# Attention's stages in another order, and score chunks of 384 and 256 keys for 512 and 128

## The chip, the cores and the metric

The kernel runs on one core of one Trainium2 chip. The metric is the device time of one execution in microseconds (us). The core's engines are TensorE (PE in the profile; its weight loads are PEld), VectorE (DVE), ScalarE (ACT), GpSimd (POOL) and the queue of SyncE (SP), which issues nearly all transfers. Each engine works its instructions strictly in the order of its program and waits on semaphores that the others raise.

## The reference, cut to what matters

One transformer block with adaptive layer norm, on x of shape 2 x 2048 x 256, in float32:

```python
mod = (silu(c) @ wmod).reshape(2, 6, 1, -1)      # sa, ca, ga, sb, cb, gb; ga and gb kept at least 0.25 in size
h = layernorm(x) * (1 + ca) + sa
k, v, q = rope(h @ Wk.T), h @ Wv.T, rope(h @ Wq.T)         # 2 query heads of 128, one shared key and value head
w = softmax(where(causal, q @ k.T * 128 ** -0.5, -inf))
x = x + ga * (concat_heads(w @ v) @ Wo.T)
h = layernorm(x) * (1 + cb) + sb
gate = softmax(h @ Wg + bg) - sigmoid(h @ Wt + bt) * 0.125
w = normalised(gate * (gate >= 0))               # 8 experts, width 1024, all computed for every token
x = x + gb * sum_e(w_e * (gelu(h @ W1_e + b1_e) @ W2_e + b2_e))
```

## The kernel before, in words

The 4096 tokens are 32 tiles of 128. SEQ lists them in the order in which attention takes them: batch 0's tiles t = 0 to 13, then batch 1's t = 0 and 1 in turn with batch 0's 14 and 15, then the rest of batch 1; i is the place in SEQ, TIME[i] its t. A product that must be near float32 is made of three matmuls on a high and a low part (hi x hi, hi x lo, lo x hi).

Attention is cut into stages (kind, i, part), and each stage into its instructions on PE, ACT, DVE and POOL:

- pre: rows and columns from wmod; wq and wo: the split weights; norm, rstd, xa, aT: layer norm of a tile, scaling, and its transposition; qkv: the projection; rope (POOL) and rotT: rotation and transposition of q and k.
- S: scores of one head against one chunk of up to 512 keys (lines 962 to 964, into one of two score banks); M (DVE, lines 1622 and 1625): the negated scores to probs with their minimum, the last chunk with the causal mask added; N: the minimum over a row's chunks; E (ACT, line 1302): the exponential of a whole row; T: transposition of probs (line 972) and its copies; PV (lines 993 to 998); O and Y: output projection and residual (line 899 and on, 1529 and on).
- xb, bT: the second layer norm and its transposition; gate (line 887): the gate's logits for four tiles, 16 matmul records of 36 columns; G1 and G2: gate weights of a batch on DVE; traw, tsum, tlo and split: tokens and weights made ready for the experts.

Which stage follows which on each engine is not written out: the planner order_stages (line 288) simulates the four engines when the program is built, with the lengths and dependencies of parts_of, and always takes the stage with the least rank:

```python
rank = (start + patience[engine].get(kind, 0), start)
```

start is when it could begin; PATIENCE holds an allowance in ns per engine and kind, the same for all tiles. A large allowance lets other stages pass. The result, ORDER, is what the engines' programs loop over (lines 917, 1274, 1562 and 1970), with waits on semaphores whose values follow from each stage's place among its kind. M of a score stage must be done before the next but one S may write its bank. SP's program keeps its own order; its stores of x1 wait for Y.

idle_fill (line 342) reads from the plan where PE would be idle for over 600 ns in the first 40 us, and puts matmuls on a zeroed part of mask_sb there (line 920), which write columns of the PV bank that nothing reads.

After attention the expert part runs 128 steps on PE (from line 1048), each with 21 products and 24 matmuls of the second layer, in an order that is written out. Three attention-side stages of the last tile, and the last gate, are done within its first steps.

Of the kernel before, what the change touches and what calls it, by code (L numbers as in the profile page):

```python
# [8 lines left out]
ACT = mybir.ActivationFunctionType  # L9
AX_X = mybir.AxisListType.X  # L10

P = 128
B, T, D = 2, 2048, 256
HS, NH = 128, 2
E, FF = 8, 1024
# [25 lines left out]
XS, PBUF, SUM_SLOTS = 8, 2, 4  # L41
# [26 lines left out]
TIME = [t for _, t in SEQ]  # L68
# [29 lines left out]
def chunks_of(i):  # L98

    return TIME[i] // 4 + 1  # L100


def width_of(i, chunk):

    return min(512, (TIME[i] + 1) * P - chunk * 512)


def stages_by_kind():
# [46 lines left out]
def parts_of(stage):  # L155


    kind, i, g = stage
# [9 lines left out]
    if kind == "split":  # L168
        end = TILES - 1
        return [("POOL", SPLIT_PHASES[g], [("rope", end, 0, "POOL", 4500), ("rotT", end, 0, "PE"),  # L170
                                           ("S", end, 4 + chunks_of(end) - 1, "PE")])]
    if kind == "pre":
        what, b = PRE[i]
        late = {"rows": 0, "gates": 1, "cols": 2}[what]
        after = [("silu", 0, 0, "DVE"), ("wmod", late, 0, "SP")]
        if PRE_AFTER[i] is not None:
            after.append(("qkv", PRE_AFTER[i], 0, "PE"))
        return [("PE", 3600 if i == 2 else 1900, after),
                ("ACT", 600, [("pre", i, 0, "PE")]) if what == "gates" else ("DVE", 900, [("pre", i, 0, "PE")])]
    if kind == "wq":  # L180
        return [("ACT", 1250, [("wqkv", 0, 0, "SP")]), ("DVE", 1150, [("wq", 0, 0, "ACT")])]
# [3 lines left out]
    if kind == "norm":  # L185
        n = ok(i + AHEAD) + ok(i - BEHIND)
        after = [("rstd", i - 2, 0, "POOL"), ("xa", i - 2 + AHEAD, 0, "DVE"), ("xb", i - 2 - BEHIND, 0, "ACT"),
                 ("Y", i - BEHIND, 0, "DVE"), ("x", i + AHEAD, 0, "SP")]
# [32 lines left out]
    if kind == "S":  # L221
        chunk = g % 4
        after = [("rotT", i, 0, "DVE")]
        n = AT[stage] - 1
        if n >= S_BANKS:
            after.append(("M", *STAGES["S"][n - S_BANKS][1:], "DVE"))
        return [("PE", 3 * max(120, 0.443 * width_of(i, chunk))  + 110 * (chunk == chunks_of(i) - 1), after)]
    if kind == "M":
        after = [("S", i, g, "PE")]
        if i >= PBUF:  # L230
# [25 lines left out]
    if kind == "G1":  # L256
# [2 lines left out]


PATIENCE = {
# [7 lines left out]
    "POOL": {"xa": 1625, "rope": 2132, "norm": 1836, "rstd": 2160, "traw": 352, "split": -1582},  # L269
}  # L270
PASS_ON = {"PE": 260, "ACT": 120, "DVE": 120, "POOL": 130, "SP": 0}
T_READER = {"T": "ACT", "aT": "DVE", "bT": "ACT"}
M_READER = {"qkv": "ACT", "Y": "DVE", "rotT": "DVE", "gate": "DVE"}
# [2 lines left out]
def reader_of(stage):  # L276

    kind, i, _ = stage
    if kind == "pre":
        return "ACT" if PRE[i][0] == "gates" else "DVE"  # L280
    if kind == "T":
        return "DVE" if is_split(stage[2]) else "ACT"
    if kind == "qkv":
        return "DVE" if TIME[i] >= EARLY else "ACT"
    return T_READER[kind] if kind in T_READER else M_READER[kind]


def order_stages(patience):

    queues, free, orders = {}, {}, {}
    ends = dict(LOADED)
    for stages in STAGES.values():
        for stage in stages:
            for engine, length, after in parts_of(stage):
                queues.setdefault((engine, stage[0]), []).append(
                    (stage, length, [x for x in after if x[:3] in AT or x[:4] in LOADED]))
                free[engine], orders[engine] = 0.0, []
    heads = {q: 0 for q in queues}  # L300
    last_in = {"T": [None] * T_BANKS, "M": [None] * M_BANKS}
    turn = {"T": 0, "M": 0}
    data_ready = {}
    while heads:
        best = None
        for (engine, kind), n in heads.items():
            stage, length, after = queues[engine, kind][n]
            if (engine, kind, n) not in data_ready:
                if any(x[:4] not in ends for x in after):
                    continue  # L310
                data_ready[engine, kind, n] = max(
                    [0.0] + [ends[x[:4]] + (PASS_ON[x[3]] if x[3] != engine else 70 * (engine != "PE"))
                             + (x[4] if len(x) > 4 else 0) for x in after])
            start = max(free[engine], data_ready[engine, kind, n])
            banks = None
            if engine == "PE":
                banks = "T" if kind in T_READER else "M" if kind in M_READER or kind == "pre" else None
            if banks:
                was = last_in[banks][turn[banks] % len(last_in[banks])]
                if was:  # L320
                    if (*was, reader_of(was)) not in ends:
                        continue
                    start = max(start, ends[(*was, reader_of(was))] + 120)
            rank = (start + patience[engine].get(kind, 0), start)
            if best is None or rank < best[0]:
                best = (rank, engine, kind, stage, start, length, banks)
        _, engine, kind, stage, start, length, banks = best
        ends[(*stage, engine)] = free[engine] = start + length
        orders[engine].append(stage)
        if banks:  # L330
            last_in[banks][turn[banks] % len(last_in[banks])] = stage
            turn[banks] += 1
        heads[engine, kind] += 1
        if heads[engine, kind] == len(queues[engine, kind]):
            del heads[engine, kind]
    return orders, ends
# [5 lines left out]
def idle_fill():  # L342

    fill, free = {}, 1000.0
    for stage in ORDER["PE"]:
        length = next(n for engine, n, _ in parts_of(stage) if engine == "PE")
        gap = ENDS[(*stage, "PE")] - length - free
        free = ENDS[(*stage, "PE")]
        if free < FILL_UNTIL and gap > 600:
            fill[stage] = int(FILL_SHARE * gap / FILL_NS)  # L350
    return fill
# [19 lines left out]
def adaln_block(nc, x, wqkvT, woT, wgt, bgt, w1, b1, w2, b2, c, wmod, cos, sin, ident, mask, out):  # L371
# [6 lines left out]
    with outer:  # L378
# [337 lines left out]
        with nc.Block() as block:  # L716
# [128 lines left out]
            def _(pe):  # L845
# [71 lines left out]
                for stage in ORDER["PE"]:  # L917
# [31 lines left out]
                    elif kind == "S":  # L949
# [6 lines left out]
                        if n >= S_BANKS:  # L956
                            pe.wait_ge(dve_M, n + 1 - S_BANKS)
                        w, b = width_of(i, chunk), BATCH[i]
                        keys = slice(chunk * 512, chunk * 512 + w)
                        q1, q2 = (q[:, i % QS, h * P:(h + 1) * P] for q in (q_hi, q_lo))  # L960
                        o = score_bank(stage)
                        nc.tensor.matmul(o[:, 0:w], q1, k_hi[b][:, keys], start=True, stop=False)  # L962
# [488 lines left out]
            def _(dve):  # L1451
# [110 lines left out]
                for stage in ORDER["DVE"]:  # L1562
# [48 lines left out]
                    elif kind == "M":  # L1611
# [3 lines left out]
                        if i >= PBUF:  # L1615
                            dve.wait_ge(*done(pe_T, "T", i - PBUF, groups_of(i - PBUF) - 1))
                        w = width_of(i, chunk)
                        to, highest = probs[i % PBUF][:, h, chunk * 512:chunk * 512 + w], top[:, i % 2, h, chunk:chunk + 1]
                        if chunk == chunks_of(i) - 1:
                            if i == 0:  # L1620
                                dve.wait_ge(l_mask, 16)
# [510 lines left out]
```

## Time and profile before

| | |
|---|---|
| median of 3 runs | 1730.13 us (1728.48 to 1731.81) |
| the profiled execution's own time | 1729.62 us |
| its span, first to last instruction | 1727.8 us |
| PE busy | 1713.5 us (99%) |
| DVE, ACT, POOL busy | 1210.5, 1012.4, 1010.5 us (70, 59, 58%) |
| mean granted clock of PE | 0.998 |

Times in the profile are from the span's start. A row of instructions gives its line, engine, operation, the tiles it writes and reads, the shape, the count, busy time and mean duration, and behind these the engine's idle time just before and who released it. PE's matmuls are pipelined: the next starts before the last one's record ends, so what a matmul costs is read from one start to the next. A float32 matmul that is not split shows as two records.

### The profile page before, as it was taken

The numbers are of one execution on the slowest core, as the hardware profiler recorded it, in microseconds if no ns is written. First come the engines' busy times: TensorE is split into PE (matmuls) and PEld (weight loads), VectorE is DVE, ScalarE is ACT, GpSimd is POOL, SyncE is SP. The second block draws the span as 40 slices with busy tenths as digits, with TensorE's granted clock in tenths as the row PEclk, the third lists the DMA queues.
The fourth block names the chain that finished last, engine by engine and source line by source line (L and its number), as shares of the span: only waits on it lengthen the run. The fifth ranks groups of instructions, "written<-read, shape, count | busy, mean of one in ns | idle before, by whom it ended". The sixth has DMA issues, their size and how long they took to land.

```text
span 1727.8 us, 26572 instructions
## 1 busy us (share of the span) xinstructions
PE 1713.5 (99%) x8416; PEld 1442.7 (83%) x8416; DVE 1210.5 (70%) x2282; ACT 1012.4 (59%) x1834; POOL 1010.5 (58%) x1722
## 2 busy tenths in 40 slices
PE   8999999999999999999999999999999999999998
PEld 7899998998888888888888888888888888888887
DVE  6787778777676666666666678666666666666676
ACT  4767777666665555555555566555555555555554
POOL 6654565355345564748483949374847566574842
PEclk9999999999999999999999999999999999999999
DMA  4100010011111111111011111222312011111101
GB/s 115 32 23 17 30 31 20 10 57 45 25 50 26 50 37 37 37 37 49 28 47 36 55 21 37 62 71 76 110 25 49 26 49 37 37 37 37 37 13 50
DMA packets 91836, 72.05 MB, mean 42 GB/s; under 512 B 11825, under 2 KB 89905, under 8 KB 91697
## 3 DMA queue, kind: packets, MB, share of 16 engines
q1 hardware_dynamic: 91552, 70.29, 14.7%
q8 instruction: 68, 1.11, 0.3%
q14 instruction: 72, 0.58, 0.1%
q10 hardware_dynamic: 144, 0.07, 0.0%
HBM read 61.82 MB, written 8.52 MB: 41 GB/s over the span
## 4 chain that ended last, share of the span: by engine, by line
PE 94%; issue 1%; ACT 1%; DVE 1%; POOL 0%; DVEq 0%; ACTq 0%; POOLq 0%
PE bank L1094 13%; PE bank L1093 13%; PE bank L1092 13%; PE bank L1048 12%; PE bank L1049 11%; PE bank L1050 11%; PE bank L972 3%; PE bank L998 3%; PE bank L1012 2%; PE bank L963 2%; PE bank L964 2%; PE bank L962 2%; PE bank L994 1%; PE bank L993 1%; PE bank L995 1%
## 5 line engine op out<-in xcount | busy, mean ns | idle before, releaser
L1381 ACT ACTIVATE g_sb<-c_sb,b_cols 128x512 f32<-128x512 f32 x384 | 276.2, 719 | 397.6 <-DVE c_sb L1896 293.7
L1721 DVE TENSOR_TENSOR h_lo<-g_sb,h_hi 128x512 fp32r<-128x512 f32 x512 | 390.6, 783 | 102.7 <-ACT h_hi L1385 102.1
L1092 PE MATMUL bank<-h_hi,w_both 128*128 128x512 f32 x1024 | 398.8, 389 | 0.0
L1094 PE MATMUL bank<-h_lo,w_both 128*128 128x512 f32 x1024 | 398.7, 389 | 0.0
L1093 PE MATMUL bank<-h_hi,w_both 128*128 128x512 f32 x1024 | 398.4, 389 | 0.0
L2060 POOL TENSOR_TENSOR h2f<-h2f,y_sb 128x256 f32<-128x256 f32 x216 | 201.5, 965 | 284.7 <-DVE y_sb L1745 284.7
L1048 PE MATMUL bank<-t_hi,w_hi 128*128 128x512 f32 x896 | 352.4, 393 | 4.1 <-DVE p_u L1887 1.8
L1049 PE MATMUL bank<-t_lo,w_hi 128*128 128x512 f32 x896 | 349.3, 390 | 0.0
L1050 PE MATMUL bank<-t_hi,w_lo 128*128 128x512 f32 x896 | 349.2, 390 | 0.0
L1385 ACT ACTIVATE h_hi<-c_sb,b_cols 128x512 fp32r<-128x512 f32 x384 | 272.2, 709 | 0.0
L1092 PEld LDWEIGHTS bank<-h_hi,w_both 128*128 128x128 f32 x1024 | 192.2, 188 | 40.1
L1094 PEld LDWEIGHTS bank<-h_lo,w_both 128*128 128x128 f32 x1024 | 192.2, 188 | 40.1
L1093 PEld LDWEIGHTS bank<-h_hi,w_both 128*128 128x128 f32 x1024 | 192.2, 188 | 40.0
L1048 PEld LDWEIGHTS bank<-t_hi,w_hi 128*128 128x128 f32 x896 | 168.4, 188 | 44.0 <-ACT p_u L1417 4.0
L1050 PEld LDWEIGHTS bank<-t_hi,w_lo 128*128 128x128 f32 x896 | 168.5, 188 | 35.3
L1049 PEld LDWEIGHTS bank<-t_lo,w_hi 128*128 128x128 f32 x896 | 168.6, 188 | 33.6
L1381 ACT ACTIVATE g_sb<-bank,b_cols 128x512 f32<-128x512 f32 x128 | 88.2, 689 | 177.6 <-PE bank L1050 177.4
L1914 DVE TENSOR_TENSOR c_sb<-bank,u 128x512 f32<-128x512 f32 x128 | 88.3, 690 | 119.1 <-PE bank L1050 116.5
L1887 DVE TENSOR_TENSOR p_u<-bank,u 128x512 f32<-128x512 f32 x128 | 88.1, 688 | 107.5 <-PE bank L1050 107.2
L1896 DVE TENSOR_TENSOR c_sb<-bank,p_u 128x512 f32<-128x512 f32 x128 | 88.5, 691 | 84.4 <-PE bank L1050 71.5
L570 POOL TENSOR_TENSOR w_sums<-w_raw 128x128 f32<-128x128 f32 x64 | 49.4, 772 | 145.6 <-PE bank L1094 131.0
L603 POOL TENSOR_TENSOR w_lo<-w_sums,w_hi 128x256 fp32r<-128x256 f32 x128 | 94.7, 759 | 0.0
(204 smaller groups left out, 2942.5 us busy)
## 6 DMA issues: line engine op xcount, KB each, us to landing
w_raw<-w_dram SPq DMA_DIRECT2D x128, 256.0 KB, 3.0
g_rows<-gates_scratch SPq DMA_DIRECT2D x31, 512.0 KB, 8.6
x_sb<-x_dram SPq DMA_DIRECT2D x32, 128.0 KB, 2.3
x_scratch<-x_sb SPq DMA_DIRECT2D x32, 128.0 KB, 1.7
x_slabs<-x_scratch SPq DMA_DIRECT2D x4, 512.0 KB, 7.3
out_dram<-x_slabs SPq DMA_DIRECT2D x4, 512.0 KB, 3.3
h2f<-x_scratch SPq DMA_DIRECT2D x4, 512.0 KB, 3.9
wmod_raw<-wmod_dram SPq DMA_DIRECT2D x4, 256.0 KB, 3.8
```

The source lines that it names most:

```text
L603: last = nc.gpsimd.tensor_tensor(lo[:, 3 + 2 * i:5 + 2 * i, :], w_sums[:, 2 * i:2 * i + 2, :], hi[:, 3 + 2 * i:5 + 2 * i, :].bitcast(F32), ...
L1048: nc.tensor.matmul(bank, hi, t_hi[p][:, b_, :], start=start, stop=False, skip_group_check=True)
L1049: nc.tensor.matmul(bank, hi, t_lo[p][:, b_, :], start=False, stop=False, skip_group_check=True)
L1050: nc.tensor.matmul(bank, lo, t_hi[p][:, b_, :], start=False, stop=stop, skip_group_check=True).then_inc(pe_prod, 1)
L1092: nc.tensor.matmul(o, w_hi, h_hi[:, ring, :], start=first, stop=False, skip_group_check=True)
L1093: nc.tensor.matmul(o, w_lo, h_hi[:, ring, :], start=False, stop=False, skip_group_check=True)
L1094: done_ = nc.tensor.matmul(o, w_hi, h_lo[:, ring, :], start=False, stop=last, skip_group_check=True)
L1381: nc.scalar.activation(g_sb[:, m % 2, :], source, ACT.Gelu_apprx_tanh, bias=bias).then_inc(act_g, 1)
L1385: nc.scalar.activation(h_hi[:, m % RING, :], source, ACT.Gelu_apprx_tanh, bias=bias).then_inc(act_hi, 1)
L1721: nc.vector.tensor_tensor(h_lo[:, m % RING, :], g_sb[:, m % 2, :], h_hi[:, m % RING, :].bitcast(F32), ALU.subtract).then_inc(dve_lo, 1)
L1896: nc.vector.tensor_tensor(c_sb[:, 0, :], bank_h, p1_u3[:], ALU.add).then_inc(dve_c22, 1)
L2060: last = nc.gpsimd.tensor_tensor(acc[:, k, half], acc[:, k, half], y_sb[:, u, k, half], ALU.add)
```

## The change

Three edits of the plan's input and one of the work:

- Chunks. For tiles with t = 4, 8, 12 the last chunk had 128 keys behind chunks of 512. The last two are now of 384 and 256 keys. Numbers of chunks, matmuls and moves stay; only where a chunk begins (first_of) and how wide it is (width_of) change.
- Allowances. PATIENCE may hold four numbers for a kind, for tiles 0 to 5, 6 to 13, 14 to 19 and 20 to 31 of SEQ. All values are new, so every engine's order may change.
- Two lengths in the planner: the third pre stage 1900 ns for 3600, and S no longer 110 ns longer for a row's last chunk.
- idle_fill stops at the first PV stage.

```diff
--- before.py
+++ after.py
@@ -100,9 +100,17 @@
     return TIME[i] // 4 + 1
 
 
+def first_of(i, chunk):
+
+    end = (TIME[i] + 1) * P
+    if end % 512 == P and end > 512 and chunk == chunks_of(i) - 1:
+        return chunk * 512 - P
+    return min(chunk * 512, end)
+
+
 def width_of(i, chunk):
 
-    return min(512, (TIME[i] + 1) * P - chunk * 512)
+    return first_of(i, chunk + 1) - first_of(i, chunk)
 
 
 def stages_by_kind():
@@ -175,7 +183,7 @@
         after = [("silu", 0, 0, "DVE"), ("wmod", late, 0, "SP")]
         if PRE_AFTER[i] is not None:
             after.append(("qkv", PRE_AFTER[i], 0, "PE"))
-        return [("PE", 3600 if i == 2 else 1900, after),
+        return [("PE", 1900, after),
                 ("ACT", 600, [("pre", i, 0, "PE")]) if what == "gates" else ("DVE", 900, [("pre", i, 0, "PE")])]
     if kind == "wq":
         return [("ACT", 1250, [("wqkv", 0, 0, "SP")]), ("DVE", 1150, [("wq", 0, 0, "ACT")])]
@@ -224,7 +232,7 @@
         n = AT[stage] - 1
         if n >= S_BANKS:
             after.append(("M", *STAGES["S"][n - S_BANKS][1:], "DVE"))
-        return [("PE", 3 * max(120, 0.443 * width_of(i, chunk))  + 110 * (chunk == chunks_of(i) - 1), after)]
+        return [("PE", 3 * max(120, 0.443 * width_of(i, chunk)), after)]
     if kind == "M":
         after = [("S", i, g, "PE")]
         if i >= PBUF:
@@ -259,15 +267,30 @@
 
 
 PATIENCE = {
-    "PE": {"aT": 853, "bT": 900, "qkv": 1076, "rotT": 985, "Y": 940, "pre": 1334, "gate": 1978, "S": 975,
-            "T": 977, "PV": 1001},
-    "ACT": {"aT": -2637, "xb": -620, "bT": -4432, "qkv": 339, "rotT": -135, "O": -1231, "norm": -794,
-            "pre": -4154, "wq": -241, "G1": 2484, "traw": 1444, "tsum": -8852, "E": 940, "T": 349},
-    "DVE": {"xa": -3943, "aT": -1508, "qkv": -1657, "rotT": -6407, "O": -1114, "Y": -1222, "norm": 94,
-            "pre": -1071, "wq": 1020, "wo": 225, "G1": -3210, "G2": -3508, "gate": -4620, "tsum": 821,
-            "tlo": -79, "M": -3080, "N": -1556, "T": -671},
-    "POOL": {"xa": 1625, "rope": 2132, "norm": 1836, "rstd": 2160, "traw": 352, "split": -1582},
+    "PE": {
+        "aT": (1046, 560, 900, 645), "bT": (826, 852, 883, 892), "qkv": (1372, 1103, 989, 947),
+        "rotT": (1000, 953, 808, 766), "Y": (678, 870, 694, 861), "pre": 1773, "gate": 1103,
+        "S": (704, 921, 911, 924), "T": (687, 911, 792, 923), "PV": (1102, 957, 926, 943),
+    },
+    "ACT": {
+        "aT": (-1903, -1575, -5842, -1993), "xb": (-6689, -6451, -7197, -1747), "bT": (791, -6967, -65, -5604),
+        "qkv": (677, 223, -111, 263), "rotT": (-2707, -915, -5797, -6565), "O": (-1251, -2912, -4427, -2595),
+        "norm": (-4257, -640, -668, 477), "pre": -827, "wq": -2526, "G1": 1457, "traw": 1955, "tsum": 832,
+        "E": (941, 1123, 584, 624), "T": (345, 531, -57, 427),
+    },
+    "DVE": {
+        "xa": (-1542, -1696, -9691, -4382), "aT": (-4742, -7023, -8155, -7911), "qkv": (-7968, -5270, -3986, -7931),
+        "rotT": (-956, -7692, -291, -5939), "O": (-172, -2897, -497, -8190), "Y": (-3563, -9531, -4252, -634),
+        "norm": (-145, 16, -281, -166), "pre": -1944, "wq": -81, "wo": 305, "G1": 701, "G2": 533, "gate": -268,
+        "tsum": 681, "tlo": -2057, "M": (-407, -5314, -490, -5831), "N": (-511, -4937, -1346, -1579),
+        "T": (-2208, -1049, -1413, -1422),
+    },
+    "POOL": {
+        "xa": (3029, 1099, 890, 992), "rope": (2037, 2012, 2177, 1842), "norm": (1776, 2173, 1664, 1360),
+        "rstd": (2047, 2937, 1703, 2080), "traw": 2206, "split": 3211,
+    },
 }
+PHASES = (6, 14, 20)
 PASS_ON = {"PE": 260, "ACT": 120, "DVE": 120, "POOL": 130, "SP": 0}
 T_READER = {"T": "ACT", "aT": "DVE", "bT": "ACT"}
 M_READER = {"qkv": "ACT", "Y": "DVE", "rotT": "DVE", "gate": "DVE"}
@@ -283,6 +306,14 @@
     if kind == "qkv":
         return "DVE" if TIME[i] >= EARLY else "ACT"
     return T_READER[kind] if kind in T_READER else M_READER[kind]
+
+
+def patience_of(patience, engine, stage):
+
+
+    kind, i, _ = stage
+    found = patience[engine].get(kind, 0)
+    return found if isinstance(found, int) else found[sum(i >= first for first in PHASES)]
 
 
 def order_stages(patience):
@@ -321,7 +352,7 @@
                     if (*was, reader_of(was)) not in ends:
                         continue
                     start = max(start, ends[(*was, reader_of(was))] + 120)
-            rank = (start + patience[engine].get(kind, 0), start)
+            rank = (start + patience_of(patience, engine, stage), start)
             if best is None or rank < best[0]:
                 best = (rank, engine, kind, stage, start, length, banks)
         _, engine, kind, stage, start, length, banks = best
@@ -343,6 +374,8 @@
 
     fill, free = {}, 1000.0
     for stage in ORDER["PE"]:
+        if stage[0] == "PV":
+            break
         length = next(n for engine, n, _ in parts_of(stage) if engine == "PE")
         gap = ENDS[(*stage, "PE")] - length - free
         free = ENDS[(*stage, "PE")]
@@ -956,7 +989,7 @@
                         if n >= S_BANKS:
                             pe.wait_ge(dve_M, n + 1 - S_BANKS)
                         w, b = width_of(i, chunk), BATCH[i]
-                        keys = slice(chunk * 512, chunk * 512 + w)
+                        keys = slice(first_of(i, chunk), first_of(i, chunk) + w)
                         q1, q2 = (q[:, i % QS, h * P:(h + 1) * P] for q in (q_hi, q_lo))
                         o = score_bank(stage)
                         nc.tensor.matmul(o[:, 0:w], q1, k_hi[b][:, keys], start=True, stop=False)
@@ -1615,7 +1648,8 @@
                         if i >= PBUF:
                             dve.wait_ge(*done(pe_T, "T", i - PBUF, groups_of(i - PBUF) - 1))
                         w = width_of(i, chunk)
-                        to, highest = probs[i % PBUF][:, h, chunk * 512:chunk * 512 + w], top[:, i % 2, h, chunk:chunk + 1]
+                        first = first_of(i, chunk)
+                        to, highest = probs[i % PBUF][:, h, first:first + w], top[:, i % 2, h, chunk:chunk + 1]
                         if chunk == chunks_of(i) - 1:
                             if i == 0:
                                 dve.wait_ge(l_mask, 16)
```

## Rows read from the trace of the kernel before

**Rows 1.** The page, part 1: busy time, share of the span, instructions.

```profile
PE 1713.5 (99%) x8416; PEld 1442.7 (83%) x8416; DVE 1210.5 (70%) x2282; ACT 1012.4 (59%) x1834; POOL 1010.5 (58%) x1722
```

**Rows 2.** Table by stretch: length, busy us of each engine, granted clock, DMA.

```profile
13.00:60.00 47.00, 42.50 (x242) 35.50 (x241) 35.22 (x114) 25.87 (x86) 37.92 (x77) 0.96 0.23 44
60.00:200.00 140.00, 140.00 (x922) 126.77 (x921) 110.44 (x349) 98.68 (x237) 72.36 (x158) 1.00 0.08 24
200.00:390.00 190.00, 189.91 (x1280) 173.15 (x1280) 146.69 (x445) 136.41 (x313) 102.37 (x230) 1.00 0.10 30
```

**Rows 3.** What PE waited for from 0 to 60 us: total, times, longest.

```profile
PE bank L907 <- DVE xa L1665: 1.7, 2, 0.9
...
PE bank L907 <- POOL xa L2001: 0.9, 1, 0.9
PE bank L1022 <- POOL rot L1992: 0.9, 1, 0.9
```

**Rows 4.** Table by stretch again, where the clock was low.

```profile
26.00:29.50 3.50, 3.12 (x11) 2.44 (x11) 2.44 (x10) 1.72 (x7) 2.62 (x10) 0.53 0.00 0
...
395.00:398.20 3.20, 3.20 (x11) 2.80 (x11) 0.72 (x3) 0.60 (x1) 3.20 (x6) 0.50 0.00 0
```

**Rows 5.** PE in order of time: start, length, count; here the filler matmuls.

```profile
19.42 1.06 PE L920 MATMUL bank<-mask_sb 128*128 128x128 f32 x8
```

**Rows 6.** Groups by shape, attention: count, busy us, mean ns.

```profile
L963 PE MATMUL bank<-k_lo,q_hi 128*128 128x128 f32 x16 | 4.4, 276 | 0.0
```

**Rows 7.** PE in order of time: score matmuls and what starts behind them.

```profile
36.93 0.33 PE L962 MATMUL bank<-k_hi,q_hi 128*128 128x384 f32 x1
...
37.46 0.60 PE L972 MATMUL bank<-ident_sb,probs 128*128 128x128 f32 x4
...
43.83 0.40 PE L962 MATMUL bank<-k_hi,q_hi 128*128 128x512 f32 x1
...
44.53 0.82 PE L972 MATMUL bank<-ident_sb,probs 128*128 128x128 f32 x6
...
49.20 0.31 PE L962 MATMUL bank<-k_hi,q_hi 128*128 128x128 f32 x1
...
49.57 0.65 PE L998 MATMUL bank<-pT,v 128*128 128x256 f32 x2
...
52.91 0.22 PE L962 MATMUL bank<-k_hi,q_hi 128*128 128x128 f32 x1
...
53.19 1.06 PE L972 MATMUL bank<-ident_sb,probs 128*128 128x128 f32 x8
...
57.25 0.28 PE L962 MATMUL bank<-k_hi,q_hi 128*128 128x256 f32 x1
...
57.61 0.28 PE L899 MATMUL bank<-wo_hi,o_hi 128*128 128x256 f32 x1
```

**Rows 8.** Groups by shape, DVE, attention: the moves of scores.

```profile
L1625 DVE TENSOR_SCALAR_CACHE_REDUCE probs<-bank 128x512 f32<-128x512 f32 x96 | 65.1, 686 | 11.7 <-PE bank L964 9.1 <-PE bank L972 2.0
...
L1622 DVE CUSTOM_DVE_ANT_0 probs<-bank,mask_sb 128x384 f32<-128x384 f32 x16 | 8.7, 550 | 0.8 <-PE bank L964 0.8
...
L1622 DVE CUSTOM_DVE_ANT_0 probs<-bank,mask_sb 128x256 f32<-128x256 f32 x16 | 6.7, 418 | 1.8 <-PE bank L964 1.8
...
L1622 DVE CUSTOM_DVE_ANT_0 probs<-bank,mask_sb 128x128 f32<-128x128 f32 x16 | 4.5, 284 | 0.5 <-issue 0.4
```

**Rows 9.** PE in order of time: the third pre stage.

```profile
24.17 1.90 PE L944 MATMUL bank<-s_rows,wmod_raw 128*128 128x64 f32 x16
```

**Rows 10.** DVE in order of time: first of G2, and what comes behind it.

```profile
384.48 0.25 DVE L1505 TENSOR_REDUCE row_a<-o_out 128x16 f32<-128x128 f32 x1
...
387.77 1.88 DVE L1643 TENSOR_TENSOR pT_lo<-bank,pT_hi 128x512 fp32r<-128x512 f32 x3
```

**Rows 11.** PE in order of time: the last gates and the first expert product.

```profile
391.29 3.65 PE L887 MATMUL bank<-wgt_sb,h2f 128*128 128x36 f32 x32
394.78 0.71 PE L1048 MATMUL bank<-t_hi,w_hi 128*128 128x512 f32 x1
```

## The prediction

> **What bounds the kernel now.** I read the page's busy table first, then a table by stretch, then what the tensor engine waited for, then its instructions one by one. The busy table puts PE at 1713.5 of 1727.8 us, no other engine above 70% [rows 1]. The table by stretch shows where the rest is [rows 2]. The expert part (from 395 us) is untouched by the diff. Of attention, 60 to 390 us holds 329.91 us of PE in 330, so a new order finds nothing to win there and can only lose; PE's waits of more than a trifle lie in 13 to 60 us, 42.50 busy of 47. Of these 4.5 us, 3.5 have a named releaser that repeats or is long [rows 3]: twice xa made on DVE (1.7 us together), xa and rot on POOL (0.9 each).
>
> Two things hide behind "busy". Between 26 and 29.5 us the granted clock was 0.53, so 3.5 x 0.47 = 1.6 us of work were lost, and between 395 and 398.2 us it was 0.50, 1.6 us more [rows 4]. Before 20.5 us PE runs filler matmuls on mask_sb while it would idle: the last eight fall at 19.42 us and take 1.06 us, hidden waiting too [rows 5]. What lies before 13 us waits for loads and the first tile's chain and keeps its order in any plan; I leave it out. So all that a better order can win in the head is 4.5 + 1.6 + 1.1 = 7.2 us.
>
> **The change, part by part.**
>
> *Score chunks.* Tiles with t = 4, 8, 12 of both batches, two heads each, make 12 pairs of chunks that go from 512 and 128 keys to 384 and 256; of the 16 score matmuls of 128 keys per source line, the other 4 are t = 0 and stay [rows 6]. What counts is start to next start over the three matmuls [rows 7]. 512 keys: 43.83 to 44.53, 0.70 us. 128 keys: 52.91 to 53.19, 0.28, or 49.20 to 49.57, 0.37. Old pair 0.98 to 1.07. 384 keys: 36.93 to 37.46, 0.53. 256 keys: 57.25 to 57.61, 0.36. New pair 0.89. The gain is 0.09 to 0.18 per pair, times 12 = 1.1 to 2.2 us; I take 1.6, the middle. It is all PE time in a stretch without PE idle, so it counts whole. Per matmul that is 0.09 to 0.12 us for 128 keys and 0.12 for 256: half the columns cost nearly as much. DVE's side is a wash: the masked move takes 686 ns for 512 (without the mask) and 284 for 128, together 0.97 us; 550 for 384 and 418 for 256 are also 0.97 [rows 8]. The number of moves, of N reductions and of ACT's exponentials stays; the first chunk now ends 0.17 us earlier (0.70 to 0.53), which lets DVE begin earlier, the second later. I cost that at nothing; DVE was busy 146.69 of 190 us in the long stretch [rows 2], and if this cover were gone, the price would be at most 0.13 us (418 less 284 ns) on the exponential of each pair, 1.6 us over the twelve.
>
> The Trainium skill's page "TensorE: Matmul & The Clock Gate" (section "Back-to-back issue gap") gives an isolated gap of N/2.4 + 2.5 ns, about 56 ns for 128 columns. By it both pairs, 640 columns in six matmuls, cost the same and this edit would be worth nothing, the sum 1.6 us later. The rows (0.09 to 0.12 us at 128) speak against it here.
>
> *New order, head.* Every stage of four engines may move, with its waits. No stage's instructions are added or dropped, DMAs and their sizes neither; SP's stores follow tile order as before, so SP moves only with the Y stages. The planner now takes 1900 ns for the third "pre" stage in place of 3600; its 16 matmuls took 1.90 us, just before the half clock at 26 us [rows 9]. The waits on DVE's xa, 1.7 us, come from xa standing among other DVE stages, which an order can mend: DVE was busy 35.22 of 47 us. The two on POOL are work: it was busy 37.92 of 47 us [rows 2], and PE stood until its last instruction of a rope or an xa. If 1.7 us of waits go, half of the clock's 1.6 may go too. Bounds: the whole 7.2 us gained; a loss of 4.5 us if the waits double. I take a gain of 1.7 + 0.8 = 2.5 us. What is late next is POOL's rope.
>
> *New order, middle.* 0 gained. ACT and DVE are idle a fifth of it or more, and POOL nearly half [rows 2], so a stage that comes one place later usually finds room. Bounds: 0 and a loss, below.
>
> *New order, end.* PE's allowance for "gate" goes from 1978 (about 1000 above S, T and PV) to 1103 (about 170 above them in the last phase), so the gates of finished quarters go out earlier. In the old tail, two of them run from 391.29 to 394.78 as 32 narrow matmuls [rows 11], and another stands a few us earlier, where DVE is in the twelve steps of G2 (384.48 to 387.77) and pT_lo of the last tile comes right behind [rows 10]. Moving gates saves nothing by itself: PE does them anyhow. If that cover goes while G2 keeps its place, PE waits up to the length of a gate, 3.65 / 2 = 1.8 us. But DVE's G2 goes from -3508 to +533 while T in the last phase stands at -1422, so T now goes ahead of G2. I take 0. The half clock at 395 us [rows 4] follows the narrow matmuls; if it hangs on them, it goes and 1.6 us are gained. No row tells whether it does, so this is a case of its own. The expert part then only starts earlier; POOL's weight split that follows the last PV begins from the same event.
>
> *Fill.* No fill after the first PV: all fills of before lie ahead of it (the last piece is that of rows 5, and FILL comes from order and lengths alone), so the break removes none of these. The new order computes its own; 0, with the head's bounds.
>
> **Sum.** Profiled time 1729.62 us (span 1727.8 and 1.8 around it), less 1.6, less 2.5: 1725.5. The median of the three runs, 1730.13, is 0.5 above the profiled one, so I forecast a median of 1726.0. A measurement can tell about 0.2% (3.5 us) from no change, so 1726.6 is the edge of "faster": the forecast stands on it.
>
> **Rivals.**
> 1. *Only the chunks.* POOL's chain sets the head, the waits change names but not their sum. For it: POOL at 81% there (37.92 of 47). Against it: 1.7 of the 4.5 us wait on DVE. 1730.1 - 1.6 = 1728.5.
> 2. *The half clock at 395 us goes as well.* For it: it follows the narrow matmuls; against: a similar stretch at 26 us has other neighbours. 1726.0 - 1.6 = 1724.4.
> 3. *The chunk edit is worth nothing*, head gain as forecast: the first matmul of 384 or 256 keys pays what the narrow one saved. 1726.0 + 1.6 = 1727.6.
> 4. *Slower: the score banks come free late.* DVE's allowance for M rises from -3080 to -407 in tiles 0 to 5 and to -490 in tiles 14 to 19, while T and Y stand there at -2208 and -3563, and at -1413 and -4252. The smaller goes first, so M, which went ahead of both (-671 and -1222 before), now goes behind them. There are two score banks, and PE's next score stage but one waits for M; its queue is in order, so T, PV and qkv behind it wait too, and with them ACT's and DVE's copies. Tiles 14 to 19 have 24 score stages. If half of them wait for one DVE move more (0.69 us, [rows 8]), that is 8.3 us: 1726.0 + 8.3 = 1734.3. It decides once DVE takes M more than about 0.7 us after its scores, a score stage's own length. Against it: DVE idles a fifth of the time, and a planned wait costs the plan as well.
>
> **Chances.** Forecast 0.42, rival 2 0.10, rival 1 0.28, rival 3 0.05, rival 4 0.15. Faster by over 0.2% takes rival 2, some four fifths of the forecast (its spread lies mostly below, since up to 7.2 us are there) and a little of the others: 0.47. Slower by over 0.2% (above 1733.6): 0.13. Within: 0.40. The range: below, all of the head and the chunks would be 1730.1 - 7.2 - 1.6 = 1721.3; above, a loss of 4.5 in the head less 1.6 gives 1733.0, with much of rival 4 left out. 1721 to 1733.
>
> **What would show it.** Chunks: 12 more matmuls of 384 keys per S line, 4 of 128 keys left of 16, L962 to L964 busy slightly less. Head: PE busy of 13 to 60 us up by 2 us, or the same work done 2 us earlier; waits on DVE's xa gone, those on rot still there. Clock: no stretch near 0.5 around the first expert product. Middle: still 0 us of PE waits from 60 to 390 us. Rival 4 would show as waits of L962 for probs L1622 or L1625. I am wrong if the first expert product (394.78 us now) starts less than 2 us or more than 7 us earlier, or if the expert part changes by over 2 us from it.

## The result

| | before | after |
|---|---|---|
| median | 1730.18 us (14 runs) | 1733.37 us (14 runs, 1730.74 to 1735.94) |
| span of the profiled execution | 1727.8 us | 1730.8 us |
| PE busy, granted clock | 1713.5 us, 0.998 | 1713.9 us, 0.997 |

The ratio is 1.0019, 95% interval 1.0012 to 1.0026: 3.2 us slower, where 4.2 us faster was forecast. The time lies 0.4 us above the stated range, and the sign was wrong.

The same table by stretch, of the kernel after (length, busy us of PE, PEld, DVE, ACT, POOL, clock, DMA), with one stretch more, from 392 to 402 us:

```profile
13.00:60.00 47.00, 41.55 (x251) 35.02 (x249) 38.00 (x117) 26.42 (x87) 37.73 (x78) 1.00 0.23 46
60.00:200.00 140.00, 139.91 (x928) 126.93 (x927) 110.44 (x345) 99.55 (x240) 73.73 (x163) 1.00 0.08 24
200.00:390.00 190.00, 188.34 (x1274) 172.36 (x1272) 143.98 (x433) 135.75 (x310) 97.67 (x219) 1.00 0.09 27
392.20:402.20 10.00, 10.00 (x39) 9.13 (x39) 6.04 (x16) 0.81 (x2) 9.71 (x19) 0.50 0.20 66
```

Against [rows 2 and 4]: in the head PE is busy 1 us less, but the half clock at 26 us is absent in this execution (clock 1.00 for 0.96). The middle has no wait. What is new lies at the end: 1.7 us of idle PE before 390 us, and 10 us of half clock (0.50 of the full 2.4 GHz, so 1.2) where there were 3.4 us. PE in order of time, after, around the last PV (the row at 387.06 is its last matmul):

```profile
383.96 1.87 PE L920 MATMUL bank<-wgt_sb,h2f 128*128 128x36 f32 x16
...
387.06 0.28 PE L1028 MATMUL bank<-pT_hi,v_lo 128*128 128x256 f32 x1
389.00 0.44 PE L940 MATMUL bank<-ident_sb,xb 128*128 128x128 f32 x2 [1.66 <-ACT xb L1297]
389.27 7.71 PE L920 MATMUL bank<-wgt_sb,h2f 128*128 128x36 f32 x48
396.79 0.77 PE L1081 MATMUL bank<-t_hi,w_hi 128*128 128x512 f32 x1
```

and its row of before:

```profile
391.17 0.28 PE L995 MATMUL bank<-pT_hi,v_lo 128*128 128x256 f32 x1
```

These give the account of the 3.0 us between the two spans. (1) Up to the last matmul of PV the new order is 391.17 - 387.06 = 4.1 us ahead. But one gate (16 narrow matmuls, 1.8 us) that stood before it now stands behind it, the chunks give 1.3 to 1.7 us (shown below), and the half clock in the head happened not to occur: a_wide, a_fix and a_fix_wide below have the same order up to there and that half clock, and their last PV starts 1.0 to 1.6 us later (388.07, 388.32 and 388.69). These three make 4.1 to 5.1 us, so nothing is left for the order of head and middle. (2) From there to the first expert product it was 394.78 - 391.17 = 3.6 us and is 396.79 - 387.06 = 9.7 us, 6.1 more: the wait for xb, 1.7; the third gate, 1.8; and 48 narrow matmuls in 7.71 us, where three gates at the pace of [rows 11] would take 5.5, so 2.2 for the clock; the remaining 0.4 is for the most part the transposition of xb itself (389.00 to 389.27), which stood ahead of the last PV before. (3) The expert part is 1730.8 - 396.8 = 1334.0 us against 1727.8 - 394.8 = 1333.0: the half clock lasts until 402.3 us there. -4.1 + 6.1 + 1.0 = 3.0.

### The profile page after: what moved, and what is told of

Its sections match the earlier page's. It is cut to its first block, busy times and chain, and to the rows that moved or that the text cites. A ratio compares the mean times of both kernels' runs of the same rounds, so it can differ in the third digit from the quotient of the medians.

```text
span 1730.8 us, 26580 instructions
## 1 busy us (share of the span) xinstructions
PE 1713.9 (99%) x8420; PEld 1444.4 (83%) x8420; DVE 1215.1 (70%) x2282; ACT 1012.7 (59%) x1834; POOL 1011.0 (58%) x1722
## 4 chain that ended last, share of the span: by engine, by line
PE 92%; issue 1%; DVE 1%; ACT 1%; POOL 1%; DVEq 0%; POOLq 0%; ACTq 0%
PE bank L1127 13%; PE bank L1125 13%; PE bank L1126 13%; PE bank L1081 12%; PE bank L1083 11%; PE bank L1082 11%; PE bank L1005 3%; PE bank L1031 3%; PE bank L1045 2%; PE bank L995 2%; PE bank L996 2%; PE bank L997 2%; PE bank L1028 1%; PE bank L1027 1%; PE bank L1026 1%
```

## The experiments

Theory 1: the loss is made at attention's end, by where the gates stand: three of them in a row behind a wait, and half clock with them. Rivals: the wait for xb alone; the new order of head and middle; the chunks. Labels beginning with a_ are made from the kernel after, with b_ from the one before. All were timed in five rounds against the kernel before, in three groups with their own executions of it; a ratio is always to those. `moved(engine, stage, behind)` takes a stage out of an engine's finished order and puts it behind another.

### What the narrow gate matmuls do to the clock: a_wide, b_wide

```diff
-matmul(bank[:, n * GATE_WIDE * NG:(n + 1) * GATE_WIDE * NG], h2_cols(...)[:, k, :], wgt_sb[:, k, :], ...)
+matmul(bank[:, n * 108:(n + 1) * 108] seen as 3 x 36, h2_cols(...)[:, k, :],
+       wgt_sb[:, k, :].unsqueeze(1).broadcast_to([P, 3, 36]), ...)
```

> The changed kernel; only its gate matmuls stream 108 columns in place of 36 (the same weights three times over). Theory 1 (the half clock from 392 to 402 us comes from three gates of narrow matmuls in a row behind a wait): the clock stays full there, the three gates take 5.3 us for 7.7 and the first expert products 2.6 us less, so 1733.4 - 5.1 = 1728.3 us, 0.9989 of the kernel before. Rival (the wait for xb at 387 us alone drops the clock, whatever the gates stream): the half clock stays and the time is 1733.4, ratio 1.0019. Rival 2 (the loss is spread over the new order's head and middle): 1733.4 as well, with the clock full at the end.

> The kernel before with the same gate matmuls of 108 columns. Theory 1: its single half-clock stretch of 3.4 us at 395 us goes, 1.7 us less, 1728.5 us, ratio 0.9990. Rival: nothing moves, 1730.2, ratio 1.0000.

a_wide: 1730.15 us, ratio 1.0000 (0.9991 to 1.0009), 3.2 us less than the kernel after. PE in order of time in a_wide, then the table by stretch of it:

```profile
389.88 0.44 PE L941 MATMUL bank<-ident_sb,xb 128*128 128x128 f32 x2 [1.52 <-ACT xb L1298]
390.15 5.51 PE L920 MATMUL bank<-wgt_sb,h2f 128*128 128x108 f32 x48
397.58 0.39 PE L933 MATMUL bank<-wo_hi,o_hi 128*128 128x256 f32 x1 [1.21 <-DVE logits L1512]
```

```profile
388.00:394.00 6.00, 4.48 (x40) 4.27 (x40) 2.20 (x6) 3.79 (x8) 5.61 (x11) 1.00 0.00 0
394.00:405.00 11.00, 9.65 (x52) 7.67 (x52) 8.82 (x22) 4.08 (x7) 8.87 (x18) 1.00 0.21 67
```

Same order, same wait for xb, 48 gate matmuls in a row: with 108 columns they take 5.51 us for 7.71, and the clock stays at 1.00. Three times the columns cost nothing, since 16 of them take 1.9 us at either width. Ten of the eleven executions of a_wide had a mean clock of 0.999 or 1.000; the kernel after had 0.997 or less in all 14. So at this place the narrow matmuls are needed for the half clock, and the wait alone does not make it. (Elsewhere it comes without a row of them: in the head, and in a_old_patience.) Of the 5.1 us expected, 3.2 came: PE arrives earlier at the last tile's projection and now waits 1.2 us for DVE, which reads the gates' logits only after G2. b_wide: 1729.66, ratio 0.9998 (0.9989 to 1.0006). The clock was 1.00 at 395 us in its profile, and none of its eleven executions was below 0.999, where 18 of the 32 of the kernel before were; but no gain in time can be told. The kernel before often has no half clock there at all: of its 32 executions beside these runs, 8 had a mean clock of 1.000, at 1728.2 to 1729.2 us, and those at 0.997 or 0.998 took 1729.1 to 1731.8.

### The same three gates in the old order: b_bunch

```diff
 ORDER, ENDS = order_stages(PATIENCE)
+moved('PE', ('gate', 4, 0), ('PV', 31, 7))
+moved('DVE', ('gate', 4, 0), ('O', 31, 0))
```

> The kernel before with gate 4 moved behind the last PV, so that three gates follow one another there, as in the changed kernel; chunks, head and middle untouched. Theory 1: PE waits up to 1.7 us for pT_lo where gate 4 stood, and the half clock grows from 3.4 to about 10 us, 3.4 us more: 1730.2 + 3.4 to 5.1 = 1733.6 to 1735.3, ratio 1.002 to 1.003. Rival (a bunch of gates is harmless): 1730.2 to 1731.9, the wait alone.

1733.85 us, ratio 1.0020 (1.0011 to 1.0029): with one gate moved, the kernel before is as slow as the kernel after. PE in order of time and the low stretch of b_bunch:

```profile
390.77 0.41 PE L918 MATMUL bank<-ident_sb,xb 128*128 128x128 f32 x2 [1.79 <-DVE pT_lo L1654]
393.46 6.64 PE L898 MATMUL bank<-wgt_sb,h2f 128*128 128x36 f32 x48
```

```profile
397.50:404.20 6.70, 6.70 (x26) 6.12 (x26) 1.24 (x4) 0.60 (x1) 3.69 (x7) 0.50 0.00 0
```

The gate had covered DVE's G2; without it PE waits 1.8 us for pT_lo, and the half clock is 6.7 us long (the profiled execution was the slowest of the eleven). Two of its eleven executions had a mean clock of 1.000: 1730.2 and 1730.4 us, which is the wait alone over the 1728.7 of the kernel before at that clock; the other nine took 1733.4 to 1735.2. That splits the price: some 1.6 us for the wait, and 3.6 us between the medians of the two groups for the clock, with the half clock of the head in it.

### Moving only what waits, or only the gates: a_spread, a_fix, a_fix_wide

```diff
 a_spread
+moved('PE', ('gate', 2, 0), ('PV', 29, 3))   # 3 behind PV 30,0; 4 behind PV 30,3; 5 behind PV 30,7; 6 behind PV 31,1
+moved('DVE', ('gate', 2, 0), ('M', 31, 1))   # 3 to 6 likewise; G1 and G2 stay last
 a_fix, a_fix_wide (this with the 108 columns)
+moved('POOL', ('norm', 32, 0), ('split', 1, 1))
+moved('ACT', ('G1', 0, 0), ('norm', 32, 0))
+moved('DVE', ('G2', 0, 0), ('G1', 0, 0))
```

> The changed kernel with its gate stages 2 to 6 moved forward on PE and DVE, one each among the scores, T and PV of tiles 29 to 31; none is left behind the last PV. Theory 1: no half clock of 10 us at the end, at most one of 3.4 us for the wait on xb, which stays (1.7 us or a little more since no gate stands behind it): 1733.4 - 3.4 to 5.1 = 1728.3 to 1730.0, ratio 0.9989 to 0.9999. Rival (the moved gates only shift PE's work and something else sets the end): 1733 to 1735, ratio 1.002 or more.

> The changed kernel with three stages moved at its end: POOL's norm of tile 30 one split phase earlier, ACT's G1 ahead of xb 30, DVE's G2 directly behind its G1. Gates and their 36 columns stay where they are. Theory 1: the wait of 1.7 us for xb is gone, but three narrow gates still follow one another and the half clock comes all the same: 1733.4 - 1.7 = 1731.7, ratio 1.001. Rival (the wait for xb is what drops the clock, so both go): 1733.4 - 1.7 - 5.1 = 1726.6, ratio 0.998.

> The same three moves and the gate matmuls of 108 columns. Theory 1: no half clock at the end, no wait for xb (1.5 us in the run with 108 columns alone) and none for the gates' logits behind G2 (1.2 us there): 1730.15 - 2.7 = 1727.4, ratio 0.9985. Rival (the waits turn into other ones, since DVE's or POOL's work is what is late): 1730.1, ratio 1.000.

All three missed. a_spread: 1734.61 us, ratio 1.0026 (1.0017 to 1.0036). No gate was left at the end, and with that no cover. It is not the clock: two of its ten executions had a mean clock of 1.000 and still took 1733.4 and 1733.5 us. What PE waited for in a_spread from 384 to 460 us (total, times, longest; the profiled execution was the slowest of the ten):

```profile
PE bank L1170 <- DVE u L1928: 2.8, 1, 2.8
PE bank L1100 <- ACT p_u L1469: 1.6, 1, 1.6
PE bank L1100 <- DVE p_u L1940: 1.2, 2, 0.7
PE bank L959 <- ACT xb L1316: 1.1, 1, 1.1
PE bank L1100 <- DVE c_sb L1949: 0.9, 1, 0.9
```

L1170 is the turning of batch 0's gates in the first expert step; it needs G2, which I had left at the end of DVE's order. a_fix: 1734.05, ratio 1.0020 (1.0012 to 1.0029); a_fix_wide: 1731.36, ratio 1.0003 (0.9995 to 1.0012). The wait for xb fell only to 1.0 us, for ACT's G1 now waited for the logits of gate 3 ahead of it, and with G2 right behind G1 the logits of gate 4 held the bank that gate 6 needs: 2.1 us in both. The half clock came again in a_fix (0.50 for 10.0 us) and not in a_fix_wide. What I took for one wait is a ring, gate 3, G1, G2, the logits' bank, that has to be moved as a whole.

### The end as a whole: a_tail, a_tail_wide

```diff
+moved('PE', ('gate', 3, 0), ('T', 31, 4))
+moved('PE', ('gate', 4, 0), ('PV', 31, 4))
+moved('DVE', ('gate', 3, 0), ('T', 31, 4))
+moved('DVE', ('G1', 0, 0), ('gate', 3, 0))
+moved('DVE', ('gate', 4, 0), ('T', 31, 7))
+moved('DVE', ('G2', 0, 0), ('gate', 4, 0))
+moved('ACT', ('G1', 0, 0), ('T', 31, 5))
+moved('POOL', ('norm', 32, 0), ('split', 1, 1))
```

> The changed kernel with its end in the order of the kernel before: gate 3 ahead of PV of tile 31, gate 4 ahead of its sixth part, G1 and G2 on DVE and ACT in between, POOL's norm of tile 30 one split phase earlier. Head and middle stay. Theory 1: two gates are left behind the last PV as before; half clock 3.4 us at most, no long wait for xb or logits: about the kernel before less the chunks, 1728 to 1729, ratio 0.999. Rival (the new order is slower in the head and middle too): 1731 or more, ratio over 1.0005.

> The same with gate matmuls of 108 columns. Theory 1: as the last or up to 1.7 us less, 1726.5 to 1728.5. Rival (DVE reads the logits behind G2, so a wait takes what the clock gives): 1729 or more.

a_tail: 1725.80 us, ratio 0.9977 (0.9965 to 0.9989). a_tail_wide: 1725.78, ratio 0.9969 (0.9957 to 0.9981). Eight moved stages out of some 1750 turn 3.2 us slower into 4 us faster; both beat either kernel, and both came out below what was expected of them. The 108 columns add nothing to it that can be told. PE in order of time in a_tail, and its stretches in the middle:

```profile
389.88 0.44 PE L957 MATMUL bank<-ident_sb,xb 128*128 128x128 f32 x2 [0.20 <-ACT xb L1314]
390.16 3.66 PE L937 MATMUL bank<-wgt_sb,h2f 128*128 128x36 f32 x32
393.65 0.48 PE L1098 MATMUL bank<-t_hi,w_hi 128*128 128x512 f32 x1
```

```profile
60.00:200.00 140.00, 139.90 (x926) 126.87 (x925) 110.28 (x346) 100.08 (x240) 73.97 (x161) 1.00 0.08 24
200.00:388.00 188.00, 188.00 (x1273) 172.22 (x1272) 144.58 (x436) 134.69 (x308) 95.83 (x215) 1.00 0.09 27
388.00:396.00 8.00, 7.79 (x62) 7.32 (x61) 5.66 (x17) 4.08 (x7) 7.51 (x14) 1.00 0.00 0
```

0.2 us of wait for 1.7, two trailing gates for three, full clock. The first expert product starts 1.1 us before that of the kernel before, and the span is 3.9 us shorter: most of the other 2.8 us are the half clock in the expert part, 1.6, and a wait of 0.8 us for p_u in its third step that is gone too. Not all of the gain is the clock: the four executions of a_tail at a mean clock of 1.000 took 1724.9 to 1725.3 us, the one of the kernel before beside them at that clock 1728.7. Half clock has not become impossible: three of a_tail's nine executions had a clock of 0.997 and took 1730.4 to 1731.7 us, and the interval holds them.

### The chunks: b_chunks, b_chunks_wide, a_old_chunks

The order of every engine stays; only the widths that the engines' programs use are the others.

```diff
 b_chunks (b_chunks_wide: with the 108 columns too)
-keys = slice(chunk * 512, chunk * 512 + w)
+keys = slice(first_of(i, chunk), first_of(i, chunk) + w)      # and probs likewise; width_of as in the change
 a_old_chunks
+def first_of(i, chunk): return min(chunk * 512, (TIME[i] + 1) * P)    # after the plan is made
```

> The kernel before with the chunk edit alone; the order of every engine stays that of the kernel before. By the prediction's sum 12 pairs x 0.13 us = 1.6 us less: about 1728.4, ratio 0.9991, and the last PV starts 1.6 us earlier (if the half clock in the head falls as before). Rival (a narrow matmul costs only its columns, so the edit is worth nothing): 1730.0 and no shift of the last PV.

> The kernel before with the chunk edit and the gate matmuls of 108 columns, order as before. If both small gains are real and add: 1.6 for the chunks and up to 1.7 for the half clock at 395 us, 1726.8 to 1728.4, ratio 0.998 to 0.999. Rival (what one gives the other takes): 1729.7 as with the 108 columns alone.

> The changed kernel's order on all engines with the old chunks of 512 and 128 keys. The chunk edit was worth 2.2 us in the kernel before; if it adds in the same way here, 1733.4 + 1.6 to 2.2 = 1735.0 to 1735.6, ratio 1.003. Rival (in the new order the chunks cost, since DVE's masked move of 256 keys comes late): 1733.4 or less.

b_chunks: 1728.05 us, ratio 0.9984 (0.9975 to 0.9992). b_chunks_wide: 1727.92, 0.9988 (0.9979 to 0.9996). a_old_chunks: 1735.57, ratio 1.0024 (1.0016 to 1.0033), 2.2 us over the median of the kernel after; but the ratios differ by 0.0005 only, 0.9 us, and their intervals overlap. Times alone thus show the edit in the old order and not surely in the new one. The traces show it in both. From the start of the first gate to that of the third, PE is fed without a break that matters. PE in order of time, these two gates in the kernel after, then in a_old_chunks:

```profile
73.96 1.95 PE L920 MATMUL bank<-wgt_sb,h2f 128*128 128x36 f32 x16
...
372.29 1.87 PE L920 MATMUL bank<-wgt_sb,h2f 128*128 128x36 f32 x16
```

```profile
74.37 1.94 PE L925 MATMUL bank<-wgt_sb,h2f 128*128 128x36 f32 x16
...
374.15 1.87 PE L925 MATMUL bank<-wgt_sb,h2f 128*128 128x36 f32 x16
```

The same stretch is 298.3 us long with the edit and 299.8 without it, 1.45 us for the ten pairs of chunks in it; five more runs of this order with the edit (a_wide, a_fix, a_fix_wide, a_tail, a_tail_wide) give 298.3 as well. In the old order it is 257.6 us without the edit (the kernel before, b_wide, b_bunch) and 256.7 to 256.8 with it (b_chunks, b_chunks_wide), 0.8 us for eight pairs. That is 0.11 to 0.15 us per pair, an estimate of 1.3 to 1.7 us for the twelve. The rest of the 2.2 us by medians is in what differs between executions: b_chunks had no half clock at 395 us in its profile, and its last PV starts 0.9 us earlier than that of the kernel before, where 1.6 were expected. The 108 columns add nothing that can be told to it. Groups by shape of the kernel after show the edit where it was counted:

```profile
L996 PE MATMUL bank<-k_lo,q_hi 128*128 128x384 f32 x28 | 9.4, 336 | 0.0
L996 PE MATMUL bank<-k_lo,q_hi 128*128 128x256 f32 x28 | 7.9, 282 | 0.0
...
L996 PE MATMUL bank<-k_lo,q_hi 128*128 128x128 f32 x4 | 1.1, 274 | 0.0
```

### The allowances: a_old_patience

```diff
-    "PE": { "aT": (1046, 560, 900, 645), ... }
+    "PE": {"aT": 853, "bT": 900, ...}            # PATIENCE as in the kernel before; the rest of the change stays
```

> The changed kernel with the old allowances, one number per kind: chunks, the planner's two lengths and the break in idle_fill stay. It is a third order; in its plan no gate stands behind the last PV and G2 comes one tile earlier. Theory 1 (the changed kernel loses at its end, and by its gates there): last PV about where it was, first expert product right behind it, no half clock of 10 us: 1726 to 1729, ratio 0.998 to 0.999. Rival (the order of the head and middle is what costs): as the changed kernel, 1733.4, since the rest of the plan is as new as there.

1737.46 us, ratio 1.0039 (1.0027 to 1.0051): slower than all others, against theory 1 as I had put it. No gate stands at its end, and yet it loses: its first expert product starts at 403.1 us, 8.3 us later than before. The middle of a_old_patience:

```profile
60.00:200.00 140.00, 139.59 (x929) 125.98 (x928) 109.33 (x338) 97.96 (x229) 69.88 (x151) 1.00 0.08 24
200.00:390.00 190.00, 186.71 (x1225) 168.36 (x1224) 147.49 (x447) 133.27 (x306) 102.11 (x219) 1.00 0.08 24
```

PE idles 3.7 us there, for 0.1 in [rows 2], 1.7 of it in one wait for pT_lo, at 386.8 us. From 388.0 to 391.5 us the clock was 0.52; the last gate, one and not three in a row, had ended at 385.1, and between the two stand that wait and transpositions of 128 columns. So a row of gates is not the only thing that half clock follows. Both together, some 5.4 us, do not cover the 8.3; where the rest goes was not found. So an order can cost several us ahead of the experts. That the old allowances fail because they were set against the old lengths of the planner, two of which the change shortened, is likely but was not tried apart. With the new allowances head and middle cost nothing against the old order; what they leave is a bad end.

## Why the prediction was wrong

*What bounds the kernel.* Right: PE, with nothing to win from 60 to 390 us and the waits in the head.

*Chunks, 1.6 us.* Right: 1.3 to 1.7 us by the starts of the gates, in both orders. By the isolated gap of the Trainium skill's page "TensorE: Matmul & The Clock Gate" (section "Back-to-back issue gap") the edit would be worth nothing; the section itself says that this gap under-counts at few columns where each matmul has a weight load. The 0.11 to 0.15 us per pair measured here do not fit the isolated gap.

*Head, 2.5 us.* Not there: this term failed too. PE's waits of 13 to 60 us went from 4.5 to 5.5 us, and they are 4.6 in a_tail, which has the same order up to there and, like the kernel before, a half clock; the waits for DVE's xa stayed. What PE waited for in the kernel after:

```profile
PE bank L940 <- DVE xa L1699: 2.0, 2, 1.1
PE bank L1055 <- POOL rot L2026: 1.6, 1, 1.6
...
PE bank L940 <- POOL xa L2035: 0.9, 1, 0.9
PE bank L1055 <- POOL rot L2024: 0.6, 1, 0.6
```

Rival 1 (POOL's chain sets the head, waits only change names) was right on this part. The half clock at 26 us, of which I counted half as won, comes and goes between executions: the profiled ones have it at 26 us (the kernel before, b_wide, b_chunks) or at 35 to 40 us (b_bunch, b_chunks_wide) with the old head, and at 34 to 42 us or not at all (the kernel after alone) with the new. It was no term to be won by an order that keeps the waits.

*End, taken as 0.* This is the step that failed. I saw that the last gates cover G2 and that half clock follows narrow matmuls, and I wrote that gates would go out earlier, since PE's allowance fell from 1978 to 1103. Only the first gate did by much (73.96 for 115.69 us). At the end the opposite happened: gate 3 went from ahead of PV of tile 31 to behind its sixth part, gate 4 behind the last. The first expert product, which was to start 2 to 7 us earlier, started 2.0 us later. A rank is a start plus an allowance against all others, and in the plan a gate also waits until the bank it writes has been read, so PE's allowance for gates cannot be read alone. The planner, worked through once more with one value set back, shows it: with PE's old allowance for gates, four of them stand behind the last PV instead of three, so that value did pull forward; with DVE's old one (-4620, now -268), or that of DVE's T, ACT's bT or POOL's norm, none stands there. These orders were not run. That T goes ahead of G2 on DVE was right, but the gate that had covered G2 and pT_lo had itself moved behind them. I had the half clock as a gain of 1.6 in rival 2 and gave its growth no case. b_bunch shows that growth and the wait at 3.5 us by the ratio (3.9 by medians) in the old kernel, a_wide shows 3.2 us of it in the new one, and a_tail, where the end is mended, comes to 1725.8: 0.2 us from the 1726.0 forecast. That is chance in part, for the head's 2.5 us are not in it; what stands in their place is the clock, with a mean of 0.999 or 1.000 in six of nine executions, and the wait for p_u. Forecast and result are 7.4 us apart: the head's 2.5 and the end's 3.5 to 3.9 are 6.0 to 6.4 of it, and some 1 us stays open.

*Rival 4 (late score banks)* did not occur: no S stage waited for M.

*Open.* Whether the new order of head and middle gives anything over the old one: a_tail (0.9965 to 0.9989) and b_chunks (0.9975 to 0.9992) overlap, and their first expert products start at 393.65 and 393.88 us, 0.2 apart, while the same instructions start up to 2.2 us apart between executions (the first gate at 115.63 to 117.86 us in the old order). Which of a_tail's eight moves are needed was not tried apart beyond a_fix, which has the move on POOL, puts G1 on ACT and G2 on DVE in other places, and wins nothing.

## What to carry to other kernels

Where one engine is busy all the time, read the seams between stages: what stands behind the last big piece of work covers the chains of the other engines, and a new order is judged by what it leaves there. Before trusting a change of allowances, print the order and look at the last thirty stages, not at the numbers that made it. Small matmuls that come in a row behind a wait can be given more columns: at 36 or 108 they take the same time at full clock, and with 108 the clock did not fall. It paid where three gates stood in a row (3.2 us from the kernel after to a_wide, 2.7 from a_fix to a_fix_wide) and gave nothing that can be told where two did (b_wide, b_chunks_wide, a_tail_wide).

## What the runs showed of the hardware

*The clock as a lottery.* The same program has executions with and without half clock: beside the first group of runs the kernel before took 1728.2 to 1729.2 us at a mean clock of 1.000 and 1729.1 to 1731.8 at 0.997 or 0.998, medians of 1728.7 and 1730.7. It is not the only thing that varies: beside the second group one execution at 1.000 took 1730.8. The stretches of half clock in these traces lasted 3 to 10 us; those at the end lie behind a wait, narrow matmuls or both. Between executions of one program with and without it the medians are 2.0 us apart in the kernel before and 3.6 in b_bunch, so a change that only alters how often it comes can move a median by that much.

*DVE held by POOL.* G2's twelve small steps took 3.3 us in the kernel before [rows 10] and 6.7 in a_fix. DVE of a_fix, and below it POOL at the same time:

```profile
388.79 0.25 DVE L1551 RECIPROCAL row_b<-row_a 128x16 f32<-128x16 f32 x1
389.08 1.38 DVE L1552 TENSOR_TENSOR o_out<-o_out,row_b 128x128 f32<-128x128 f32 x1
...
392.61 1.24 DVE L1557 SCALAR_TENSOR_TENSOR weights<-o_out 128x128 f32<-128x128 f32 x1
```

```profile
389.04 1.26 POOL L2059 TENSOR_TENSOR t_lo<-h2f,t_hi 128x512 fp32r<-128x512 f32 x1
...
392.39 1.31 POOL L2059 TENSOR_TENSOR t_lo<-h2f,t_hi 128x512 fp32r<-128x512 f32 x1
```

A step with two SBUF inputs that takes 0.29 us elsewhere lasts to the end of POOL's instruction (390.46 and 390.30 us; 393.85 and 393.70). By the Trainium skill, "SBUF — State Buffer" (Terms), the two share a port pair, and the loser waits for the whole instruction of the other; the rows agree. In the kernel before POOL had only small steps at that time. A chain of small DVE steps is best put where POOL has no tensor work.
